# The third normalisation from group sums of the gated chunk and of its squares, gate times deviation spread once, and the last part re-staged over five rounds

## The chip, the cores and the metric

One core of one Trainium2 chip. The metric is the device time of one execution in microseconds; lower is better.

## The reference, cut to what matters

The input is 256 images of 256 channels on 7 x 7 positions. Four layers follow one another, each of them added to its input:

```python
x = x + _L0_conv_ref(_gn(x), ...)     # 1x1 convolution with gathered weights
x = x + _L1_conv_ref(_gn(x), ...)     # linear attention with a depthwise convolution
x = x + _L2_conv_ref(_gn(x), ...)     # spatial gate per group of 8 channels
x = x + _L3_conv_ref(_gn(x), ...)     # attention over the 49 positions of an image
```

`_gn` normalises every group of 8 channels of an image over its 8 x 49 values (32 groups, eps 1e-5). The change concerns the last two layers. The gate of the third one, for the normalised input v of a group: s is the sum of v over the 8 channels, the position of its maximum gives a vector q, and

```python
sim = (q . v) * D * zero + (mean over positions of v . v) * one
ctx = (sim - sim.mean()) / (sim.std(ddof=1) + 1e-05) * weight + bias
out = v * sigmoid(ctx)                # D: a gaussian around the maximum's position
```

The fourth layer, for its normalised input xf of an image (256 x 49):

```python
f, g, hh = Wq xf, Wk xf, Wv xf        # 32, 32 and 256 rows
beta = softmax(f^T g, axis=0)
out = gamma[0] * (hh beta) + xf
```

## The kernel before, in words

The kernel has a set-up, a phase for the first two layers (up to about 1588 us of the span, not touched) and `gate_and_attention_phase` (line 941), which does the last two. The first phase stores the normalised input of the gate layer (z2) in DRAM and keeps, per image and group, its mean (`gate_mean`), its standard deviation (`gate_std`) and its mean over the positions (`gate_gap`).

The last phase works on 16 chunks of 16 images. A chunk lies as 128 channels x 2 halves (t or m) x 784 columns (16 images x 49 positions). Group values lie in rows: 128 partitions stand for 4 quarters of the chunk x 32 groups, with 4 images x 49 = 196 columns. PE makes such rows from a chunk with 0/1 matrices (`sel`, "group sum": 8 matmuls) and spreads them back over the channels with `spread` (4 matmuls per half).

The phase is a software pipeline written out by hand. Every engine runs a loop of rounds (`rounds`); in round r a step with age k works on chunk r - k. The lists `v_round` (DVE), `pe_round`, `a_round` (ACT), `g_round` (POOL) and `sp_round` (SP, the queue of loads and stores) set the order of the steps on each engine; semaphores (`wait`, `done`) order the engines against each other. A step that waits holds everything behind it on its own engine. `v_then` makes a DVE step wait for its own result before the next one starts.

A chunk's way, with ages 0 to 6, so 22 rounds for 16 chunks: load z2 (0); group sums and search of the maximum (1, `pe_sums`, `v_find`); spread of the one-hot row, `v_picked`, `v_qv`, `v_prod` (2); the group sum of prod, `v_sim`, POOL's square root by a power (`g_deviation`), `v_context` (L1159 to L1163), tanh, `v_gate` (L1169), `v_gated` (L1173), `v_x3` (L1178), its sum per image and channel (`v_sum`, L1184) (3). Then the third normalisation, from x3 itself: `pe_mean` sums 8 channels (L1324), `v_centre` (L1188, L1192) subtracts the mean, ACT squares, `v_square_sum` (L1198) sums, `pe_var` (L1330), `v_var` (L1203), POOL's `g_root` on 128 x 32 values (L1511), `v_scale` (L1211) gives z3 (4 to 5). Then attention (5 to 6): `pe_fg`, `pe_scores`, `v_max` (L1220), exponentials on ACT, `v_probs` (L1227, L1228), `pe_turn`, `pe_hh`, `pe_out`, which adds z3 with an identity matmul (L1376, L1379), and `v_x4` (L1235), which adds x3 for the two halves m (x4a, x4b). SP stores the chunk.

POOL's other step is `g_gapped` (L1499), a product of a chunk with one value per image.

## Time and profile before

| | us |
|---|---|
| median of 3 runs | 2079.17 (2075.14 to 2084.48) |
| the profiled execution | 2083.96 |
| its span, first to last instruction | 2082.1 |
| the last phase in it | from about 1588 to 2082 |

Shares of the span: PE 86%, DVE 66%, ACT 43%, POOL 13%. These are means over three phases with different limits; the rows below are taken from the last phase alone. A busy time is the time in which the engine has an instruction in work; an instruction that is held inside its execution counts as busy, so a mean above the usual one for its size is a sign of holding. PEclk is the granted share of PE's clock. A row's "idle ... <-" names what ended the engine's idle time before it. Lines are those of the kernel before; tiles are named without their number, so z stands for z2 and z3 and x for x3 and x4.

### The profile page before, as it was taken

The page shows a single profiled execution, that of the slowest core. Times are in us where ns is not written, and L with a number is a line of the kernel's source. Part 1 is how long each engine was busy: PE and PEld are TensorE (multiplying, and loading weights), DVE is VectorE, ACT ScalarE, POOL GpSimd, SP SyncE. Part 2 cuts the span into 40 slices and gives each one's busy share as a digit, 9 for nine tenths or more (in the row PEclk, how much of TensorE's full clock was granted, in tenths as well). Part 3 has the DMA queues.
Part 4 walks back from the last instruction along what each step waited for, and adds up shares of the span by engine and source line. Part 5 has one row for each costly group of instructions (what it writes and reads, how often), then busy time and mean ns, then how long its engine had stood idle before and what let it go on. Part 6 is the DMA issues. An engine that isn't in the chain of part 4 may idle for free. (4 is left out here: it accounts for less than half of the span.)

```text
span 2082.1 us, 42128 instructions
## 1 busy us (share of the span) xinstructions
PE 1786.3 (86%) x16164; PEld 1195.1 (57%) x16164; DVE 1372.3 (66%) x2786; ACT 901.7 (43%) x2341; POOL 277.0 (13%) x189
## 2 busy tenths in 40 slices
PE   2699999999999999997877888999983499999998
PEld 1355555555555555565555666666661366666666
DVE  4677777666555556442333447777875899999994
ACT  0344454454554544453433445455541144444343
POOL 1000000001111101002111110000001233333331
PEclk9899999999999999998988899999995699999999
DMA  3112222237666667479988986545513001111101
GB/s 100 39 63 78 101 94 78 78 125 185 207 170 199 201 160 215 145 185 218 237 231 219 246 229 166 134 121 149 156 48 128 16 32 63 62 63 63 47 32 47
DMA packets 199916, 267.17 MB, mean 128 GB/s; under 512 B 108516, under 2 KB 159588, under 8 KB 199720
## 3 DMA queue, kind: packets, MB, share of 16 engines
q1 hardware_dynamic: 189320, 225.68, 38.4%
q10 hardware_dynamic: 10240, 38.54, 6.0%
q8 instruction: 132, 2.16, 0.4%
q14 instruction: 64, 0.52, 0.1%
q0 software_dynamic: 160, 0.26, 0.0%
HBM read 148.84 MB, written 115.61 MB: 127 GB/s over the span
## 5 line engine op out<-in xcount | busy, mean ns | idle before, releaser
L499 DVE TENSOR_TENSOR vk<-p_vk,mask_vo 128x512 f32<-128x512 f32 x256 | 176.4, 689 | 478.3 <-PE p_vk L392 478.3
L426 PE MATMUL p_dw<-tw,q 98*64 98x98 f32 x3072 | 198.3, 266 | 86.8 <-ACT agg_out L694 34.9
L834 POOL COPY q<-qd 98x768 f32<-98x768 f32 x128 | 110.5, 900 | 1085.5 <-DMA qd<-qkv_scratch 787.2
L667 ACT ACTIVATE half_b<-p_qkv 98x384 f32<-98x384 f32 x256 | 134.2, 524 | 244.2 <-PE p_qkv L351 229.6
L426 PEld LDWEIGHTS p_dw<-tw,q 98*64 98x64 f32 x3072 | 148.1, 143 | 151.5 <-issue 67.8
L694 ACT ACTIVATE agg_out<-p_dw 128x294 f32<-128x294 f32 x256 | 106.9, 417 | 258.6 <-PE p_dw L426 246.0
L452 PE MATMUL p_g<-o,w_proj 128*128 128x392 f32 x512 | 207.5, 531 | 3.4 <-DVE var L555 2.8
L351 PE MATMUL p_qkv<-w_qkv,half_a 128*98 128x384 f32 x512 | 193.8, 502 | 6.7 <-DVE half_a L571 6.7
L351 PE MATMUL p_qkv<-w_qkv,z_odd 128*98 128x384 f32 x512 | 190.2, 494 | 1.8 <-DVE z_odd L571 1.8
L404 PE MATMUL p_out<-vk,qr 128*49 128x136 f32 x2048 | 170.5, 287 | 8.5 <-DVE oN L514 5.4
L711 ACT ACTIVATE o<-p_turn 128x196 f32<-128x196 f32 x256 | 85.5, 334 | 167.5 <-PE p_turn L413 166.1
L1360 PE MATMUL p_b<-wv,z 128*98 128x256 f32 x512 | 121.2, 385 | 8.0 <-DVE x L1235 8.0
L413 PE MATMUL p_turn<-ident,oN 128*128 128x128 f32 x512 | 111.1, 300 | 19.1 <-ACT qr L686 17.4
L673 ACT ACTIVATE vT<-half_b,image_of 98x256 f32<-98x256 f32 x256 | 124.4, 538 | 0.0
L404 PEld LDWEIGHTS p_out<-vk,qr 128*49 128x49 f32 x2048 | 110.3, 125 | 24.3 <-issue 10.0
L452 PEld LDWEIGHTS p_g<-o,w_proj 128*128 128x128 f32 x512 | 91.8, 199 | 56.2 <-issue 16.8
L392 PEld LDWEIGHTS p_vk<-vT,kT 98*32 98x32 f32 x4096 | 71.6, 109 | 89.4 <-issue 85.0
L392 PE MATMUL p_vk<-vT,kT 98*32 98x66 f32 x4096 | 114.2, 228 | 3.4 <-DVE vk L503 3.2
L514 DVE TENSOR_TENSOR oN<-p_out,rden 128x256 f32<-128x256 f32 x256 | 108.6, 424 | 8.8
L351 PEld LDWEIGHTS p_qkv<-w_qkv,half_a 128*98 128x98 f32 x512 | 81.0, 174 | 57.4 <-issue 47.0
L351 PEld LDWEIGHTS p_qkv<-w_qkv,z_odd 128*98 128x98 f32 x512 | 79.8, 171 | 50.7 <-issue 44.9
L673 ACT ACTIVATE vT<-p_qkv,image_of 98x256 f32<-98x256 f32 x256 | 106.9, 474 | 0.0
(192 smaller groups left out, 3202.4 us busy)
## 6 DMA issues: line engine op xcount, KB each, us to landing
qkv_scratch<-half_b SPq DMA_DIRECT2D x32, 1176.0 KB
qd<-qkv_scratch SPq DMA_DIRECT2D x64, 588.0 KB
agg_scratch<-agg_out ACTq DMA_DIRECT2D x128, 294.0 KB, 5.8
tw<-in_w_toep SPq DMA_DIRECT2D x128, 220.5 KB
half_a<-agg_scratch SPq DMA_DIRECT2D x48, 392.0 KB, 6.9
half_b<-agg_scratch SPq DMA_DIRECT2D x48, 392.0 KB, 6.8
half_a<-in_x SPq DMA_DIRECT2D x16, 784.0 KB, 4.9
x_scratch<-xb SPq DMA_DIRECT2D x16, 784.0 KB, 4.8
```

The costliest lines, as they stand in the source:

```text
L351: mm = pe.matmul(p_qkv[r][0:PR, 0:QKV], z[c % 2][:, t, PR * w:PR * w + PR], W["w_qkv"][:, t, QKV * e:QKV * e + QKV], start=(t == 0), stop= ...
L392: mm = pe.matmul(p_vk[32 * c:32 * c + 32, 2 * VC * pr:2 * VC * pr + 2 * VC], kT[:, G % 2, pr, 32 * c:32 * c + 32], vT[:, G % 2, pr, :, c, ...
L404: mm = pe.matmul(out_of[64 * i:64 * i + S, pr, 0:VO], qr[:, G % 4, at:at + S], vk[:, G % 2, pr, i, :], start=True, stop=True)
L413: mm = pe.transpose(turned_of[:, pr, 0:128], oN[:, G % 2, pr, :], W["ident"][:, :])
L426: mm = pe.matmul(p_dw[NP * cp:NP * cp + NP, PR * s:PR * s + PR], q2[:, U % Q2, DB_CH * cp + 3 * (f % DB_FILLS) + s, :, :].rearrange("r w q ...
L452: mm = pe.matmul(bank[:, 0:HALF], W["w_proj"][:, q0 + e, 128 * m:128 * m + 128], o[:, n % 2, e, HALF * h:HALF * h + HALF], start=(e == 0), ...
L499: v.tensor_tensor(dst[:, :, 0:128].rearrange("p k (c n) -> p k c n", c=HC), src[:, :, 0:2 * D].unsqueeze(2).to_broadcast([128, 4, HC, 2 * D]),
L514: v.tensor_tensor(oN[:, G % 2, :, :].rearrange("p r (h d) -> p r h d", h=8), out_of[:, :, 0:128].rearrange("p r (h d) -> p r h d", h=8), r ...
L667: a.activation(raw[:, e, g % 4, :, r], p_qkv[r][0:PR, 0:QKV], ACT.Copy).then_inc(raw_ev, 1)
L673: a.activation(vT[:, G % 2, :, i, :, 0:2 * D], src.rearrange("r q (c n) -> r q c n", c=HC), ACT.Copy, scale=W["image_of"][:, i:i + 1]).the ...
L834: g.tensor_copy(q2[:, U % Q2, DB_CH * cp:DB_CH * cp + DB_CH, :, :].rearrange("r n w q -> r w n q"), qd[:, :, at:at + DB_CH, :]).then_inc(q ...
L1360: mm = pe.matmul(p_b[0:PR, n % 2, C * q:C * q + C], two_images(z3[it % Z3S][:, t, :], 2 * n + q), wv[:, t, :], start=(t == 0), stop=(t == ...
```

## The change

- The gated chunk's mean and variance per group are no longer taken from x3. As v * sigmoid + mean has the form (gate x z2) / 2 + constant inside a group, its moments are sums of gate x (group sum of z2) and gate^2 x (group sum of z2^2). ACT squares z2 at age 0 (`a_square`), `pe_sums` sums z2 and the squares, POOL weighs both rows (`g_weighed`), DVE sums them per image (`v_moment`) and makes the variance in group rows (`v_var`, 128 x 4), POOL takes the power (`g_root`, 128 x 4).
- The gate is multiplied with the reciprocal deviation in group rows (`v_gate_r`) and spread once; `v_zg` multiplies z2 by it. POOL adds a shift per image and channel (`g_shift`), which gives z3. The shift and the deviation come from `v_coef_rows`, one matmul pair (`pe_coef`) and `v_coef`.
- x3 is not kept. The residual of the fourth layer, x3 + z3, is zg x (1 + deviation) + base: half 0 on POOL (`g_rest`), half 1 on ACT in 16 short activations (`a_rest`). The identity matmuls leave `pe_out`.
- The softmax's reciprocal times gamma is a DVE step on 98 x 8 (`v_share`), the product is POOL's (`g_probs`).
- `pe_spread` and `pe_scores` use 64 rows of the array per matmul, alternating between the two halves of the rows. `sstd_eps` becomes a SCALAR_TENSOR_TENSOR with a tile of 1e-5.
- The ages are 0 to 4, with the store at 5: 21 rounds. All five lists have a new order. Four more constants are loaded ahead of the rounds.

The core of the diff (the rewritten operand forms of `v_find`, `v_dist` and `v_sim`, which keep their work, are left out, as are the declarations):

```diff
-    Z2S, X3S, Z3S = 5, 3, 3
+    Z2S, Z3S, ROWS = 6, 3, 4
...
         def v_context(v, it):
             wait(v, "sstd", it + 1)
-            v_then(v, it, v.tensor_scalar(sstd_eps[:, :], sstd[:, :], float((S - 1) ** -0.5), 1e-5,
-                                          ALU.mult, ALU.add), "sstd_eps")
+            v_then(v, it, v.scalar_tensor_tensor(sstd_eps[:, :], sstd[:, :], float((S - 1) ** -0.5), eps[:, :],
+                                                 ALU.mult, ALU.add), "sinv", 0, 2)
...
+        def v_moment(v, it):
+            wait(v, "weighed", 2 * it + 2)
+            done(v.tensor_reduce(moment[:, :, :].rearrange("g k b -> g (k b)"),
+                                 weighed[:, :, :].rearrange("g k (b s) -> g (k b) s", b=NQ), AX.X, ALU.add), "moment")
+        def v_var(v, it):
+            n = GS * S
+            wait(v, "moment", it + 1)
+            wait(v, "coef_rows", 2 * it)
+            v_then(v, it, v.tensor_scalar(mean[:, :], moment[:, 0, :], 0.5 / n, None, ALU.mult), "var_raw", 0, 3)
+            v_then(v, it, v.tensor_tensor(mean2[:, :], mean[:, :], mean[:, :], ALU.mult), "var_raw", 1, 3)
+            v_then(v, it, v.scalar_tensor_tensor(var[:, :], moment[:, 1, :], 0.25 / n, mean2[:, :],
+                                                 ALU.mult, ALU.subtract), "var_raw", 2, 3)
+            done(v.tensor_scalar(var[:, :], var[:, :], 0.0, 1e-5, ALU.max, ALU.add), "var_ok")
+        def v_gate_r(v, it):
+            wait(v, "rstd_ok", it + 1)
             wait(v, "gate_mm", 2 * it)
+            done(v.scalar_tensor_tensor(g_image(gate_r[:, :]), g_image(gate[:, :]), 0.5, g_over(rstd[:, :]),
+                                        ALU.mult, ALU.mult), "gate_r")
+        def v_coef_rows(v, it):
+            wait(v, "rstd_ok", it + 1)
+            wait(v, "coef_mm", it)
...
+            v_then(v, it, v.tensor_tensor(std[:, :], var[:, :], rstd[:, :], ALU.mult), "std", 0, 2)
+            v_then(v, it, v.tensor_tensor(rstd_of[:, :, :], by_quarter(rstd[:, :]), quarter[:, :, :], ALU.mult), "std", 1, 2)
+            done(v.scalar_tensor_tensor(coef_rows[:, 0, :, :], by_quarter(mean[:, :]), -1.0, rstd_of[:, :, :],
+                                        ALU.mult, ALU.mult), "coef_rows")
+            done(v.scalar_tensor_tensor(coef_rows[:, 1, :, :], by_quarter(std[:, :]), 1.0, quarter[:, :, :],
+                                        ALU.add, ALU.mult), "coef_rows")
+        def v_coef(v, it):
+            wait(v, "coef_mm", it + 1)
...
+            v_then(v, it, v.tensor_copy(c[:, :, :, :].rearrange("p t k b -> p (t k b)"), p_stat[:, 0:2 * KT * NB]), "coef", 0, 2)
+            done(v.tensor_tensor(base[it % 2][:, :, :], c[:, :, 0, :], W["gate_mean"][:, it, :, :], ALU.add), "coef")
-        def v_gated(v, it, t):
+        def v_zg(v, it, t):
             wait(v, "gate_mm", 2 * it + t + 1)
-            done(v.scalar_tensor_tensor(by_half(gx[:, t, :]), rows, 0.5, by_half(z2[it % Z2S][:, t, :]),
-                                        ALU.mult, ALU.mult), "gated")
+            done(v.tensor_tensor(by_half(zg[it % Z3S][:, t, :]), by_half(z2[it % Z2S][:, t, :]), rows, ALU.mult), "zg")
...
-            done(v.scalar_tensor_tensor(sc[:, :, :, :], sc[:, :, :, :], W["gamma"][0:PR, 0:1], over(srec[:, :, :]),
-                                        ALU.mult, ALU.mult), "probs")
+            done(v.tensor_scalar(share[:, :, :], srec[:, :, :], W["gamma"][0:PR, 0:1], None, ALU.mult), "share")
...
         def pe_spread(pe, sel_rows, src, t, name):
-            for q in range(4):
-                mm = pe.matmul(p_rows[:, q // 2, QC * (q % 2):QC * (q % 2) + QC], sel_rows[:, t, q, :], src[:, :],
-                               start=True, stop=True)
+            for q in (0, 2, 1, 3):
+                h = q // 2
+                mm = pe.matmul(p_rows[:, h, QC * (q % 2):QC * (q % 2) + QC], sel_rows[64 * h:64 * h + 64, t, q, :],
+                               src[64 * h:64 * h + 64, :], start=True, stop=True)
...
+        def pe_coef(pe, it):
+            wait(pe, "coef_rows", 2 * it + 2)
+            for t in range(KT):
+                mm = pe.matmul(p_stat[:, 2 * NB * t:2 * NB * t + 2 * NB], spread_all[:, t, :],
+                               coef_rows[:, :, :, :].rearrange("g k q b -> g (k q b)"), start=True, stop=True)
+            done(mm, "coef_mm")
...
         def pe_out(pe, it, m):
             for h in range(2):
                 wait(pe, "bt_ev", 2 * it + h + 1)
-                pe.matmul((p_a, p_b)[m][:, h, 0:HALF], W["ident"][:, :], z3[it % Z3S][:, m, HALF * h:HALF * h + HALF],
-                          start=True, stop=False)
...
+        def a_rest(a, it, part):
+            if part == 0:
+                wait(a, "shifted", 2 * it + 2)
+                wait(a, "coef", 2 * it + 2)
+            for b in range(NB // 4 * part, NB // 4 * part + NB // 4):
+                cols = zg[it % Z3S][:, 1, S * b:S * b + S]
+                done(a.activation(cols, cols, ACT.Identity, bias=base[it % 2][:, 1, b:b + 1],
+                                  scale=coef[it % 2][:, 1, 1, b:b + 1]), "rest_b")
...
+        def g_shift(g, it, t):
+            wait(g, "zg", 2 * it + t + 1)
+            wait(g, "coef", 2 * it + 1)
+            wait(g, "hh_mm", 4 * (it + 1 - Z3S))
+            done(g.tensor_tensor(by_b(z3[it % Z3S][:, t, :]), by_b(zg[it % Z3S][:, t, :]),
+                                 b_over(coef[it % 2][:, t, 0, :]), ALU.add), "shifted")
+        def g_rest(g, it):
+            cols = by_b(zg[it % Z3S][:, 0, :])
+            wait(g, "coef", 2 * it + 2)
+            done(g.tensor_tensor(cols, cols, b_over(coef[it % 2][:, 0, 1, :]), ALU.mult), "rest_a")
+            wait(g, "rest_a", 2 * it + 1)
+            done(g.tensor_tensor(cols, cols, b_over(base[it % 2][:, 0, :]), ALU.add), "rest_a")
...
-            run(g_root, 6)
-            run(g_deviation, 4)
-            run(g_gapped, 2)
+            run(g_deviation, 2)
+            run(g_shift, 3, 1)
+            run(g_weighed, 2)
+            run(g_root, 2)
+            run(g_gapped, 0)
+            run(g_rest, 3)
+            run(g_probs, 3)
+            run(g_shift, 2, 0)
...
-            for r in range(chunks + 6):
+            for r in range(chunks + 5):
```

The whole of `v_x3`, `v_sum`, `v_centre`, `v_square_sum` and `v_scale` is removed. The new order of a round, each step with its age and its half or part:

- DVE: var 3; picked 2, half 1; coef_rows 3; max 4; gate_r 3; qv 2; coef 3; prod 2; share 4; dsum 2; zg 3, half 0; sim 2; hot 1; ssq 2; zg 3, half 1; dist 1; context 2; picked 1, half 0; gate 2; x4 4, half 0; find 0; x4 4, half 1; moment 2.
- PE: turn 4; sums 0; hot 1, half 0; out 4, both halves; fg 3; hot 1, half 1; hh 3, part 0; scores 3; hh 3, part 1; coef 2; hh 3, part 2; gate 2, half 0; hh 3, part 3; sim 1; gap 0; gate 2, half 1.
- SP: load 0; store 5 (before: store 6, load 0).

## Rows read from the trace of the kernel before

**Rows 1.** Windows: stretch, its length, busy us of each engine (instructions), PEclk, DMA.

```profile
1746.33:1773.53 27.20, 24.70 (x183) 17.83 (x182) 26.68 (x40) 11.21 (x34) 10.00 (x3) 1.00 0.18 61
```

**Rows 2.** Timelines of PE and DVE: start, us, engine, line, op, out<-in, count, idle.

```profile
1598.74 1.53 PE L1274 MATMUL p_sum<-z,sel 128*32 128x196 f32 x16 [2.61 <-DMA z<-z_scratch]
...
1693.92 0.97 DVE L1235 TENSOR_TENSOR x<-p_b,x 128x784 f32<-128x784 f32 x1
...
1993.11 0.97 DVE L1235 TENSOR_TENSOR x<-p_b,x 128x784 f32<-128x784 f32 x1
...
2077.34 0.97 DVE L1235 TENSOR_TENSOR x<-p_b,x 128x784 f32<-128x784 f32 x1 [2.13 <-PE p_b L1379]
```

**Rows 3.** Groups by form, 1740 to 1900, DVE: busy us, mean ns | idle before.

```profile
L1211 DVE TENSOR_TENSOR z<-zc,rstd 128x784 f32<-128x784 f32 x12 | 11.6, 968 | 0.0
...
L1159 DVE TENSOR_SCALAR sstd_eps<-sstd 128x4 f32<-128x4 f32 x6 | 11.4, 1905 | 0.0
L1192 DVE TENSOR_TENSOR zc<-x,mean 128x1568 f32<-128x1568 f32 x6 | 10.8, 1792 | 0.2
L1184 DVE TENSOR_REDUCE stat<-x 128x32 f32<-128x1568 f32 x6 | 10.7, 1786 | 0.2
L1178 DVE TENSOR_TENSOR x<-gx,gate_mean 128x1568 f32<-128x1568 f32 x6 | 10.7, 1783 | 0.0
L1198 DVE TENSOR_REDUCE stat<-sq 128x32 f32<-128x1568 f32 x6 | 10.7, 1778 | 0.0
...
L1228 DVE SCALAR_TENSOR_TENSOR sc<-sc,gamma,srec 98x784 f32<-98x784 f32 x6 | 6.2, 1034 | 0.2
```

**Rows 4.** The same view, small steps of DVE.

```profile
L1169 DVE TENSOR_TENSOR gate<-tanh,one_std 128x196 f32<-128x196 f32 x6 | 2.2, 359 | 0.0
...
L1105 DVE TENSOR_TENSOR below<-last,row_ends 128x24 f32<-128x24 f32 x6 | 1.1, 176 | 0.0
```

**Rows 5.** Timelines of POOL and DVE in the first rounds, POOL beside DVE.

```profile
1603.31 3.00 DVE L1099 TENSOR_TENSOR hot_exact<-hot,last 128x196 bf16<-128x196 f32 x1
...
1621.05 2.81 POOL L1499 TENSOR_TENSOR gapped<-z,gate_gap 128x1568 f32<-128x1568 f32 x1
...
1621.09 2.79 DVE L1159 TENSOR_SCALAR sstd_eps<-sstd 128x4 f32<-128x4 f32 x1 [0.29 <-POOL sstd L1505]
...
1667.06 2.82 POOL L1499 TENSOR_TENSOR gapped<-z,gate_gap 128x1568 f32<-128x1568 f32 x1
...
1667.46 4.06 DVE L1192 TENSOR_TENSOR zc<-x,mean 128x1568 f32<-128x1568 f32 x1
```

**Rows 6.** POOL's powers: timeline of a late round, and the group by form.

```profile
2000.90 5.43 POOL L1511 TENSOR_TENSOR rstd<-var,minus_half 128x32 f32<-128x32 f32 x1 [5.47 <-DVE var L1203]
...
2004.30 1.04 DVE L1228 SCALAR_TENSOR_TENSOR sc<-sc,gamma,srec 98x784 f32<-98x784 f32 x1
...
L1505 POOL TENSOR_TENSOR sstd<-ssq,plus_half 128x4 f32<-128x4 f32 x6 | 6.0, 1007 | 72.9 <-DVE ssq L1155 72.9
```

**Rows 7.** Timeline of PE and its weight loads (PEld) in steady rounds.

```profile
1741.78 0.85 PE L1376 MATMUL p_a<-z,ident 128*128 128x392 f32 x2
1742.14 1.19 PEld L1379 LDWEIGHTS p_a<-beta,hh 98*128 98x128 f32 x8
...
1743.33 0.85 PE L1376 MATMUL p_b<-z,ident 128*128 128x392 f32 x2
...
1760.43 1.56 PE L1281 MATMUL p_rows<-gate,spread 128*128 128x196 f32 x8
```

**Rows 8.** Timeline of PE, then the window around it (columns as rows 1).

```profile
1639.52 0.38 PE L1324 MATMUL p_stat<-stat,mask 128*128 128x32 f32 x2 [3.83 <-DVE sim L1143]
...
1639.00:1642.00 3.00, 0.96 (x10) 0.75 (x14) 2.43 (x7) 0.68 (x2) 0.57 (x1) 0.63 0.00 0
```

**Rows 9.** Groups by form, 1740 to 1900, ACT.

```profile
L1436 ACT ACTIVATE tanh<-sim,half_par 128x196 f32<-128x196 f32 x6 | 3.3, 550 | 3.9 <-DVE sim L1163 3.9
```

**Rows 10.** Timeline of SP, constant loads ahead of the rounds.

```profile
1591.65 0.43 SPq L1554 DMA_DIRECT2D wqk<-in_wqk  x1
```

More of the change, by code:

```diff
@@ L968, in gate_and_attention_phase @@
         pick = sb("pick", [128, KT, COLS])
-        gx = sb("gx", [128, KT, COLS])
         gapped = sb("gapped", [128, KT, COLS])
-        zc = sb("zc", [128, KT, COLS])
         sq = sb("sq3", [128, KT, COLS])
-        stat = sb("stat3", [128, 2, KT * NB])
-        mean = sb("mean3", [128, KT, NB])
-        var = sb("var3", [128, KT * NB])
-        rstd = sb("rstd3", [128, KT, NB])
+        sums = [sb(f"sums_{i}", [128, 2, QC]) for i in range(ROWS)]
+        gate2 = sb("gate2", [128, QC])
+        weighed = sb("weighed", [128, 2, QC])
+        moment = sb("moment", [128, 2, NQ])
+        mean = sb("mean3", [128, NQ])
+        mean2 = sb("mean2", [128, NQ])
+        var = sb("var3", [128, NQ])
+        rstd = sb("rstd3", [128, NQ])
+        std = sb("std3", [128, NQ])
+        rstd_of = sb("rstd_of", [128, 4, NQ])
+        coef_rows = sb("coef_rows", [128, 2, 4, NQ])
+        coef = [sb(f"coef_{i}", [128, KT, 2, NB]) for i in range(2)]
+        base = [sb(f"base_{i}", [128, KT, NB]) for i in range(2)]
+        gate_r = sb("gate_r", [128, QC])
         qv = sb("qv", [128, KT, NB])
@@ L1029, in gate_and_attention_phase @@
         p_b = ps("p_b", [128, 2, 512])
-        names = """consts params logged std_mm met_sp met_g
-            s_mm s_ev gapped gap_mm gap_ev best at_best counted last hot below row col apart dist2 gauss dsum
-            hot_mm picked qv prod sim_mm sim_max sim ssum sim_centred sim_squared ssq sstd sstd_eps sinv context
-            tanh gate_ok gate_mm gated x3 sum_ok mean_mm mean_ok centred squared square_sum var_mm var_ok rstd_ok z3
-            fg_mm fg_ev score_mm smx neg_max exp srec probs hh_mm hh_ev bt_mm bt_ev o_mm x4a x4b""".split()
+        names = """consts params logged std_mm met_sp
+            sq_ok s_mm s_ev gapped gap_mm gap_ev found last hot placed apart gauss dsum
+            hot_mm picked qv prod sim_mm sim sim_centred sim_squared ssq sstd sinv context
+            tanh gate_ok gate2 weighed moment var_raw var_ok rstd_ok gate_r std coef_rows coef_mm coef
+            gate_mm zg shifted rest_a rest_b fg_mm fg_ev score_mm neg_max exp share probs hh_mm hh_ev
+            bt_mm bt_ev o_mm x4a x4b""".split()
         sems = {name: sem("p2_" + name) for name in names}
@@ L1304, in pe_hot @@
             if t == 0:
-                wait(pe, "gated", 2 * it - 2)
+                wait(pe, "zg", 2 * it - 2)
             else:
@@ L1311, in pe_gate @@
         def pe_gate(pe, it, t):
-            wait(pe, "gate_ok", it + 1)
+            wait(pe, "gate_r", it + 1)
             if t == 0:
@@ L1316, in pe_gate @@
             else:
[L1317 to L1330 removed]
+                wait(pe, "zg", 2 * it + 1)
+            pe_spread(pe, spread, gate_r, t, "gate_mm")
+        def pe_coef(pe, it):
[4 more added lines that the diff above has]
+            done(mm, "coef_mm")
         def pe_fg(pe, it):
[L1333 removed]
+            wait(pe, "shifted", 2 * it + 2)
             wait(pe, "x4a", it)
@@ new lines, in a_fg, with a_exp @@
+        def a_fg(a, it, h):
+            wait(a, "fg_mm", it + 1)
+            wait(a, "score_mm", it)
+            for k, dst in enumerate((f_sb, g_sb)):
+                done(a.activation(dst[2 * G * h:2 * G * h + G, :], p_a[2 * G * h + G * k:2 * G * h + G * k + G, 0, 0:HALF],
+                                  ACT.Copy), "fg_ev")
+        def a_exp(a, it, h):
+            wait(a, "neg_max", 2 * it + 2)
+            wait(a, "bt_mm", 2 * it)
+            wait(a, "share", 2 * it - 1)
+            for q in range(4):
+                done(a.activation(sc[:, h, q, :], scores[:, h, q, :], ACT.Exp, bias=neg_max[:, h, q:q + 1],
+                                  accum_out=ssm[:, h, q:q + 1]), "exp")
```

318 lines of the change are left out of this document (152 added, 166 removed).

## The prediction

> **What bounds the kernel now.** I read the windows by stage first, then the starts of one step that comes once a round, then the groups of instructions by form, and last the timelines of VectorE (DVE) and GpSimd (POOL) side by side. The change touches only the third phase. In a steady round of it DVE is busy 26.68 of 27.20 us, TensorE (PE) 24.70, ScalarE (ACT) 11.21, POOL 10.00, and the granted clock is 1.00, the 2.4 GHz level [rows 1]. So DVE sets the pace, and PE is only 10% behind it.
>
> The phase is a pipeline. The second half of a chunk's output (x4b) is the last step of the chunk. Its first start is 1693.92, the twelfth 1993.11, the sixteenth 2077.34; the first group sums start at 1598.74 [rows 2]. So the first chunk needs 95.2, eleven steady rounds take 299.2 (27.20 each), the four last rounds 84.2, and 4.8 remain to the end of the span at 2082.1: 1598.7 + 95.2 + 299.2 + 84.2 + 4.8 = 2082.1. I make the new sum in these five terms.
>
> **What leaves DVE.** Per round: x3 (1.78), its sum (1.79), the centring (1.79), the sum of squares (1.78), two scalings (2 x 0.97), the product with the softmax's reciprocal (1.03, now POOL's) [rows 3], and two steps on 128x32, taken at 0.18 as the 128x24 step [rows 4]: 10.5. A further loss is hidden in L1159: a TENSOR_SCALAR on 128x4 takes 1.905 on average [rows 3], against some 0.17 for its size [rows 4], so 1.74 of it is waiting; that is taken up below.
>
> **What comes to DVE.** Eleven steps on 4 to 64 elements (four for mean and variance, four for the coefficient rows, two for the coefficients, one for the softmax share) at 0.18 = 2.0; gate_r, 196 elements, 0.36 [rows 4]; the moment, 392 elements, between 0.36 (196) and 0.97 (784) [rows 3, 4], 0.56 by interpolation. Together 2.9. The gated product stays at its price. So DVE's own work is 26.68 - 1.74 - 10.5 + 2.9 = 17.3, and 18.0 with 0.7 for the gaps that steps waiting for their predecessor leave (0.5 in the round of before [rows 1], with more such steps now).
>
> **What DVE then waits for.** The rows show that POOL and DVE stop each other. gapped ran 1667.06 to 1669.88; the centring, which reads two SBUF operands, started at 1667.46 and took 4.06 instead of 1.79, so it ended 1.64 after gapped. And when the pow ended at 1621.05, gapped started at 1621.05 and the DVE step that waited for the pow at 1621.09: it took 2.79 [rows 5]. POOL's pow does not hold DVE: a 1.04 step with two SBUF operands ran at 2004.30 inside a pow of 5.43 [rows 6].
>
> The Trainium skill, "SBUF — State Buffer", section "Who interferes with whom", says the same and more: the port pair that both share is an exclusive lock, held for the whole instruction, and a DVE instruction with two SBUF inputs contends for it with a GpSimd instruction that reads SBUF. It speaks against this change, which gives POOL seven more such instructions a round. On gapped the trace agrees (4.06 for 1.79), on the pow it does not (1.04 inside 5.43). By the rule without that exception the two pows of a round would hold DVE too, up to 2.0 more; the sum goes by the rows.
>
> The new POOL work: two shifts, the rest's multiply and add, the softmax product (784 elements each), two weighings (196). gapped has 1568 elements at 2.82 [rows 5]; half of it is 1.41. With a fixed cost per instruction, 0.37 from the two pow sizes (1.007 for 4 columns, 5.43 for 32) [rows 6], it is 1.60. I take 1.45, near the plain half, as gapped is the same kind of step. The pow of the root falls from 5.4 (32 columns) to 1.0 (4 columns). POOL's round is then some 13, never the bound by itself.
>
> The Trainium skill, "GPSIMD Engine Reference", section "3.1 Elementwise — side-by-side cycle accounting", gives two-input steps about 2.6 cycles an element, which is an estimate of 1.70 for 784 elements; by it gapped would take 3.40, and the row has 2.82. With 1.70 the round below would be about 0.9 longer.
>
> Now the order of the new round. DVE starts with the four variance steps (to 0.9), POOL takes the root (0.9 to 1.9), and right behind it in its queue gapped (1.9 to 4.7), then the rest's multiply and add. DVE meanwhile takes picked and comes to std, which reads var and rstd and waits for the root: it becomes ready at the very moment gapped starts, as the step at 1621.09 did, and is held 2.8. Its two successors each wait for the one before, POOL gets in between with 1.45 each. That group costs 5.6 whichever of the two wins a tie. Later shift 0 meets the centring of sim (0.7), shift 1 the row search (1.1), the second weighing the find (0.2). Stalls: 7.6. Where DVE waits for ACT or PE (best for the sums, ssq for the squares, the mean for the moment) I count 1.2. **Round: 18.0 + 7.6 + 1.2 = 26.8, taken as 26.9.** The new DVE wait on the root holds everything behind it on DVE: max, gate_r, qv, prod; and PE's coef, which holds hh 2, gate 0, hh 3 and sim.
>
> **What lies beside it.** PE: the identity matmuls of the output go (0.85 of a group that begins every 1.55; the eight weight loads of 1.19 stay and pace the rest [rows 7]), 4 x 0.36 = 1.4 saved; the group sum of the squares comes, 1.53 at the half clock [rows 2], so 0.8: 24.1; that two small matmul pairs become one I leave out. Whether matmuls on two halves of the array's rows run together no row shows; if the two gate groups of 1.56 [rows 7] did, PE would be at 22.6, if they gained nothing 24.1. DVE's 26.9 covers both. ACT: 16 short activations with two per-partition operands and the squares of the gate, at most 0.55 each as tanh, which has two such operands and 196 elements where most of these have 49 [rows 9], and the longer sums 0.2: at most 11.2 + 9.6 = 20.8. Covered; if DVE's round fell below that it would show. SP: four more constant loads ahead of the first chunk, at most 0.43 each [rows 10]: +1.6 once. The z load waits for zg instead of gated, six buffers deep, and the store now stands behind the load in SP's queue; with the load's wait five chunks back neither is late.
>
> **The sum.** The first chunk: x4b came in the seventh round, after six rounds in 95.2 (15.9 each); it now comes at the end of the fifth: 5 x 15.9 = 79. Start 1598.7 + 1.6; first chunk 79; eleven rounds of 26.9 = 296; the four last rounds 84, taken as before, since fewer chunks are in flight there and PE's work keeps nearly its size; 4.8. Together **2066**, 16 under the span of 2082.1. The profiled execution itself took 2083.96, which is 4.8 above the median of the runs, 2079.17; 16 less than that median is **2063**. Most of the gain is the shorter pipeline, little of it the 9 us that DVE is spared.
>
> **Rivals.**
> 1. *DVE's short steps slip past POOL* (four elements held for 2.8 are shown only for a TENSOR_SCALAR, not for a step with two tensors). Then DVE needs 19.2 and PE paces the round at 22.6 to 24.1: 1600.3 + 72 + 11 x 23.3 + 79 + 4.8 = 2012 for the span (a stall of some 1.4 less in each of the first five rounds, and PE's saving in the last four), about 2009 for the median, and 1995 or less if the hot and score groups, split in the same way, gain too. For: a step that small was never seen against gapped in the two-operand form. Against: the centring's 4.06, the 3.00 of a two-operand step of 196 elements that is otherwise near 0.36, and 2.79 for four elements [rows 5].
> 2. *A longer hold or a slower clock eats the rest.* With 1.60 a POOL step the round is 27.6. And PE idles 3 to 4 us before coef (in the order above its hh 1 ends near 4, the coefficient rows come near 7.8): in the trace an idle of 3.83 stands before a window with a mean granted clock of 0.63, part of it at the 1.2 GHz level [rows 8]; that would put sim and gate some 1.5 later, to 28.4. Median 2068 to 2082: no measurable change.
> 3. *Slower: all of POOL's shared-port time lands on DVE.* POOL's steps that hold the port sum to 2.8 + 5 x 1.45 + 2 x 0.4 = 10.9. If POOL's next step always goes before a waiting DVE step, and each meets one, the round is 18.0 + 10.9 + 1.2 = 30.1: 1600.3 + 79 + 331 + 84 + 4.8 = 2099, median about 2095. It decides against the change from 29.5 a round on (2092.5, which is 10.4 over 2082.1). For: POOL's steps are spread over the whole DVE queue. Against: DVE spends about 9 us of the round in eight steps that read PSUM or reduce (seven of 784 elements, one of 1568, at the prices of rows of that size [rows 3]), and some POOL time must fall there.
>
> **How the numbers follow.** Forecast (2052 to 2068) 0.45; rival 1 and what lies between it and the forecast 0.22; rival 2 0.20; rival 3 0.13. The likeliest is 2063. The range takes rival 1 from 1995 and rival 3's lower part, to 2090, leaving about 1 in 10 outside on each side. What a measurement of this kernel can tell from no change is about 0.5% (10.4 us). Faster by more: forecast and rival 1, 0.67; within: rival 2, 0.20; slower: rival 3, 0.13.
>
> **What would show it.** In the changed kernel's profile: std, four elements, with a mean near 2.8 and the next two near 1.4, means the hold is as told; near 0.2 means rival 1. x4b spaced 26.9 in steady rounds, the first 79 after the first group sums. POOL's 784-element steps between 1.41 and 1.60 where DVE does not hold them. PE's gate groups at 0.8 or 1.56 tell whether the halves run together. A granted clock under 1.00 in steady rounds speaks for rival 2, a round of 29.5 or more for rival 3. The prediction fails at its root if DVE is no longer the engine that the round waits for.

## The result and the profile after

The changed kernel takes 2058.51 us (median of 6 runs, 2052.93 to 2064.51), the kernel before, beside it on the same chip, 2079.35 (6 runs, 2073.96 to 2084.48): a ratio of 0.9914, 95% interval 0.9889 to 0.9940. The prediction was 2063, range 1995 to 2090. The profiled execution of after took 2054.89, with a span of 2053.1.

The five terms of the prediction's sum, read from the same starts as in [rows 2]. Timeline of after: start, us, engine, line, operation, out<-in, what ended the idle before.

```profile
1589.71 1.54 PE L1296 MATMUL p_sum<-z,sel 128*32 128x196 f32 x16 [2.65 <-DMA z<-z_scratch]
...
1664.38 0.98 DVE L1259 TENSOR_TENSOR x<-p_b,zg 128x784 f32<-128x784 f32 x1
...
1965.14 0.96 DVE L1259 TENSOR_TENSOR x<-p_b,zg 128x784 f32<-128x784 f32 x1
...
2048.23 0.97 DVE L1259 TENSOR_TENSOR x<-p_b,zg 128x784 f32<-128x784 f32 x1 [0.81 <-PE p_b L1398]
```

| term, us | before | predicted | after |
|---|---|---|---|
| first group sums to first x4b | 95.2 | 79 | 74.7 |
| eleven steady rounds | 299.2 | 296 | 300.8 |
| last four rounds | 84.2 | 84 | 83.1 |
| to the end of the span | 4.8 | 4.8 | 4.9 |
| the whole stretch | 483.4 | 464 | 463.4 |

The stretch is 20.0 shorter (483.4 - 463.4), and the medians differ by 20.8. All of it is the first term, 20.5; a steady round is not shorter but 0.14 longer: 27.34 (300.8 / 11) for 27.20. The two spans differ by 29, 9 of which lie before 1589.71, in code that the change doesn't touch; the first group sums move that much from execution to execution (they start at 1588.5 to 1604.2 in the traces of this document), so kernels are compared here from their first group sums on, or by medians.

A steady round of after, windows (columns as in [rows 1]: stretch, length, then PE, PEld, DVE, ACT, POOL, the granted clock and DMA): the whole round, then one window of 1 us in it.

```profile
1773.70:1801.00 27.30, 22.02 (x188) 15.48 (x188) 24.68 (x44) 16.59 (x52) 13.48 (x10) 0.94 0.17 60
...
1784.70:1785.70 1.00, 1.00 (x4) 0.58 (x3) 1.00 (x1) 1.00 (x6) 0.00 (x0) 0.50 0.03 8
```

Against [rows 1], DVE is busy 24.68 instead of 26.68, PE 22.02 instead of 24.70, ACT 16.59 instead of 11.21, POOL 13.48 instead of 10.00, and the granted clock is 0.94, with a stretch at 0.50, the 1.2 GHz level. No engine is full, and the round is as long as before. Where it goes is in the same round's timelines of POOL, DVE and PE:

```profile
1776.99 2.82 POOL L1536 TENSOR_TENSOR gapped<-z,gate_gap 128x1568 f32<-128x1568 f32 x1
1779.77 1.50 POOL L1573 TENSOR_TENSOR zg<-zg,coef 128x784 f32<-128x784 f32 x1
1781.35 1.53 POOL L1575 TENSOR_TENSOR zg<-zg,base 128x784 f32<-128x784 f32 x1
...
1777.05 2.78 DVE L1218 TENSOR_TENSOR std<-var,rstd 128x4 f32<-128x4 f32 x1 [0.26 <-POOL rstd L1554]
1779.86 1.44 DVE L1219 TENSOR_TENSOR rstd_of<-rstd,quarter 128x16 f32<-128x16 f32 x1
1781.34 0.17 DVE L1220 SCALAR_TENSOR_TENSOR coef_rows<-mean,rstd_of 128x16 f32<-128x16 f32 x1
1781.43 1.48 DVE L1222 SCALAR_TENSOR_TENSOR coef_rows<-std,quarter 128x16 f32<-128x16 f32 x1
...
1790.71 0.42 DVE L1158 SCALAR_TENSOR_TENSOR sim<-p_stat,half_zero,dsum 128x196 f32<-128x196 f32 x1 [1.16 <-issue]
...
1782.96 0.63 PE L1349 MATMUL p_stat<-coef_rows,spread_all 128*128 128x32 f32 x4 [3.45 <-DVE coef_rows L1222]
1783.43 3.32 PE L1381 MATMUL p_b<-wv,z 128*98 128x256 f32 x8
...
1787.81 1.97 PE L1381 MATMUL p_b<-wv,z 128*98 128x256 f32 x8
...
1791.17 0.93 PE L1304 MATMUL p_rows<-gate_r,spread 64*128 64x196 f32 x8
```

Read the starts and the ends: std (4 elements) ends with gapped, rstd_of (16) ends with the rest's multiply, the second coefficient row with the rest's addition. These three take 5.70 where 0.5 would do. PE's coef waits 3.45 for the last of them; behind that wait the clock is 0.50, the next hh group takes 3.32 instead of 1.97, and DVE waits 1.16 before sim. So a chain that starts with a POOL instruction of no urgency comes back to DVE 13 us later.

### The profile page after: what moved, and what is told of

Its sections match the earlier page's. It is cut to its first block and busy times, and to the rows that moved or that the text cites. A ratio compares the mean times of both kernels' runs of the same rounds, so it can differ in the third digit from the quotient of the medians.

```text
span 2053.1 us, 42896 instructions
## 1 busy us (share of the span) xinstructions
PE 1729.0 (84%) x16292; PEld 1150.4 (56%) x16292; DVE 1331.2 (65%) x2851; ACT 988.1 (48%) x2613; POOL 335.9 (16%) x301
## 5 line engine op out<-in xcount | busy, mean ns | idle before, releaser
L452 PE MATMUL p_g<-o,w_proj 128*128 128x392 f32 x512 | 201.7, 518 | 3.4 <-DVE var L555 2.9
L1381 PE MATMUL p_b<-wv,z 128*98 128x256 f32 x512 | 144.7, 433 | 16.5 <-DVE x L1259 16.0
L1381 PEld LDWEIGHTS p_b<-wv,z 128*98 128x98 f32 x512 | 88.5, 183 | 52.1 <-issue 24.9
```

Source lines behind the costliest of these rows:

```text
L452: mm = pe.matmul(bank[:, 0:HALF], W["w_proj"][:, q0 + e, 128 * m:128 * m + 128], o[:, n % 2, e, HALF * h:HALF * h + HALF], start=(e == 0), ...
L1381: mm = pe.matmul(p_b[0:PR, n % 2, C * q:C * q + C], two_images(z3[it % Z3S][:, t, :], 2 * n + q), wv[:, t, :], start=(t == 0), stop=(t == ...
```

## The experiments

Theory A is: POOL's long two-operand instructions hold (stop and lengthen) DVE's steps that have two SBUF operands or are a TENSOR_SCALAR, and this sets the round; the gain of the change is the shorter passage of the first chunk alone. Each expectation sets its own theory B against it. Rounds are the distances of x4b in the traces.

**e1: POOL waits for the coefficient rows before gapped.**

```diff
             wait(g, "gap_mm", it)
+            wait(g, "coef_rows", 2 * it - 2)
```

> One edit: POOL waits for both coefficient rows of the chunk two back before it starts gapped. Now gapped runs 2.8 right behind the root, and std, rstd_of and the second coefficient row take 2.78, 1.44 and 1.48 on DVE instead of some 0.17 each: 5.2 of a round of 27.34. Theory A (POOL's instruction holds DVE, and with it PE's coef): the three fall to 0.2 or less, PE's wait of 3.45 before coef is gone and the granted clock of a steady round is back at 1.00, and DVE's wait of 1.16 before sim goes too. Part returns, because gapped then runs beside the maximum (0.96, reads PSUM) and meets neg_max and gate_r, 1.8 at most, and the rest's two steps meet base and prod, 1 at most. Round 27.34 - 5.2 - 1.2 + 1.8 + 1 = 23.7 to 25.5, first chunk 5 to 6 shorter, median about 2010 to 2032. Theory B (the hold is only handed on: whichever two-operand step comes next takes all of gapped): neg_max or gate_r takes 2.8, the round stays between 26.5 and 28, median within 10 of 2058.

Measured: median 2034.12, ratio to before 0.9769 (0.9726 to 0.9811). Seven of the eleven rounds take 25.0 to 25.3, four 26.3 to 27.0 (mean 25.7, just above theory A's 25.5); the median lies 2 above its range. Timeline of DVE, POOL and PE of e1:

```profile
1769.17 0.16 DVE L1218 TENSOR_TENSOR std<-var,rstd 128x4 f32<-128x4 f32 x1 [0.26 <-POOL rstd L1555]
...
1769.67 0.17 DVE L1222 SCALAR_TENSOR_TENSOR coef_rows<-std,quarter 128x16 f32<-128x16 f32 x1
...
1770.79 2.07 DVE L1243 TENSOR_SCALAR neg_max<-smx 98x8 f32<-98x8 f32 x1
...
1770.01 2.82 POOL L1537 TENSOR_TENSOR gapped<-z,gate_gap 128x1568 f32<-128x1568 f32 x1 [0.87 <-DVE coef_rows L1222]
...
1785.42 3.73 PE L1398 MATMUL p_a<-beta,hh 98*128 98x98 f32 x16
...
1811.85 2.03 PE L1398 MATMUL p_a<-beta,hh 98*128 98x98 f32 x16
```

The three steps take 0.16 to 0.17, and PE's wait before coef is gone. A wait added to POOL takes 2.0 to 2.4 off the seven short rounds. There is a second effect: in every round PE now waits 1.9 before the group sums, because ACT's eviction of gap_sim comes late. In the long round read closely the output group behind that wait took 3.73 at the low clock; in the short round after it, behind the same wait, it took 2.03. The granted clock is back at 1.00, as theory A had it, in only three of the eleven rounds. Theory B, that the hold is merely handed on, holds in part: neg_max takes 2.07, to the end of gapped, and sim's second step 1.78 instead of 0.53.

**e2: rstd_of doesn't wait for std.**

```diff
-            v_then(v, it, v.tensor_tensor(std[:, :], var[:, :], rstd[:, :], ALU.mult), "std", 0, 2)
+            done(v.tensor_tensor(std[:, :], var[:, :], rstd[:, :], ALU.mult), "std")
```

> One edit: rstd_of no longer waits for std, which it doesn't read. Theory A (the prediction's step: the successor of a held step is held again because it waits for its predecessor, and POOL gets in between): rstd_of follows std at once and takes 0.17 to 0.2; 1.3 of its 1.44 goes, round 26.1 if nothing takes its place, or the hold moves to the first coefficient row, which still waits (0.18 to 1.4, round unchanged within 0.3). Theory B (POOL's next instruction already stands ready and goes before DVE's next one, wait or no wait, as the second coefficient row, which waits for nothing, was held 1.48): rstd_of stays at 1.4, round 27.3.

Measured: median 2044.04, ratio 0.9837 (0.9799 to 0.9876); every round 26.2. Timeline of e2, from two rounds:

```profile
1771.28 2.78 DVE L1218 TENSOR_TENSOR std<-var,rstd 128x4 f32<-128x4 f32 x1 [0.26 <-POOL rstd L1554]
1773.98 0.16 DVE L1219 TENSOR_TENSOR rstd_of<-rstd,quarter 128x16 f32<-128x16 f32 x1
1774.17 1.36 DVE L1220 SCALAR_TENSOR_TENSOR coef_rows<-mean,rstd_of 128x16 f32<-128x16 f32 x1
1775.46 0.16 DVE L1222 SCALAR_TENSOR_TENSOR coef_rows<-std,quarter 128x16 f32<-128x16 f32 x1
...
1783.02 1.78 DVE L1161 TENSOR_TENSOR sim<-sim,gap_sim 128x196 f32<-128x196 f32 x1
...
1809.62 0.42 DVE L1158 SCALAR_TENSOR_TENSOR sim<-p_stat,half_zero,dsum 128x196 f32<-128x196 f32 x1 [0.77 <-issue]
1810.08 0.93 DVE L1161 TENSOR_TENSOR sim<-sim,gap_sim 128x196 f32<-128x196 f32 x1
```

Without its wait rstd_of follows the held std at once and passes; the next step, which waits, lets POOL in. So the prediction's "POOL gets in between" is right for rstd_of. It is not a rule for every step that waits: in after the first coefficient row waits for rstd_of too, and starts 0.01 before POOL's addition (1781.34 against 1781.35), with 0.17. The hold moved to the first coefficient row, as theory A allowed, but the round didn't stay the same: the second row then passed, which the expectation hadn't said. Of three holds two are left, PE's wait before coef is 1.95 instead of 3.45, and in the round shown the granted clock is 1.00 and the wait before sim is gone. Part is taken back at once: sim's second step now meets the softmax product and the shift on POOL, 1.78 instead of 0.53. In four of the eleven rounds the clock does fall behind coef's wait (mean 0.93). There DVE waits 0.72 to 0.77 before sim, and the hold of the second step is as much shorter (0.92 to 0.98), since it ends with the shift on POOL: these rounds take 26.2 as well.

**e3 and e6: filler matmuls in PE's wait before coef, eight and five.**

```diff
+            wait(pe, "picked", min(2 * it + 4, 2 * chunks))
+            for k in range(8):
+                pe.matmul(p_rows[:, 0, 0:HALF], W["ident"][:, :], z2[it % Z2S][:, 0, 0:HALF], start=True, stop=True)
             wait(pe, "coef_rows", 2 * it + 2)
```

> One edit: eight matmuls of 392 columns, whose result nobody reads, fill the wait of PE before coef (3.45 idle, after which the granted clock is 0.50 to 0.57 for about 3 and PE's next three groups take some 1.7 longer). Theory A (the low clock is the cause of DVE's wait of 1.16 before sim): the granted clock of a steady round returns to 1.00, that wait falls under 0.2, the round is 26.1 to 26.4, median about 2043 to 2048. Theory B (the low clock is covered, the wait before sim comes from the late coefficient rows): wait and round stay within 0.3 of 1.16 and 27.34. If the filler itself runs past the coefficient rows, coef starts up to 0.5 later.

Measured for e3: median 2071.36, ratio 0.9960 (0.9939 to 0.9982), rounds 27.33. The filler ran 5.43, past the coefficient rows: coef came 1.7 late, so the wait of 1.07 before sim, with the clock at 1.00, can't tell the theories apart. The 13 more than after lie in the first passage (77.1) and the last four rounds (94.0). e6 repeats it with `range(5)`.

> The changed kernel with five filler matmuls in PE's wait before coef instead of eight: the eight took 5.43 and made coef 1.7 late, so that DVE's wait before sim stayed at 1.07 although the granted clock was back at 1.00. Five take 3.4, the length of the wait. Theory A (the low clock makes DVE wait before sim): clock 1.00, that wait under 0.2; the round falls, but as in e2 the second step of sim may then meet POOL's softmax product and shift (1.78 for 0.53), so between 26.1 and 27.3. Theory B: the wait stays near 1.16 with the clock at 1.00.

Measured for e6: median 2066.61, ratio 0.9922 (0.9895 to 0.9949), rounds 27.3 to 27.4, just above the range given; the 8 more than after lie in the last four rounds (92.5 for 83.1). Timelines of PE and DVE of e6, then windows of 1 us:

```profile
1789.50 3.45 PE L1348 MATMUL p_rows<-z,ident 128*128 128x392 f32 x10
...
1793.56 1.95 PE L1384 MATMUL p_b<-wv,z 128*98 128x256 f32 x8
...
1803.48 1.40 PE L1296 MATMUL p_sum<-z,sel 128*32 128x196 f32 x16 [1.90 <-ACT gap_sim L1439]
...
1799.60 0.42 DVE L1158 SCALAR_TENSOR_TENSOR sim<-p_stat,half_zero,dsum 128x196 f32<-128x196 f32 x1
1800.05 1.79 DVE L1161 TENSOR_TENSOR sim<-sim,gap_sim 128x196 f32<-128x196 f32 x1
```

```profile
1794.00:1795.00 1.00, 1.00 (x6) 0.75 (x6) 1.00 (x3) 0.83 (x5) 0.00 (x0) 1.00 0.00 0
...
1804.00:1805.00 1.00, 1.00 (x19) 0.83 (x15) 0.93 (x4) 0.11 (x1) 1.00 (x2) 0.50 0.00 0
```

With the clock held at 1.00 behind coef the hh group takes 1.95 and DVE no longer waits before sim: the low clock was the cause of that wait. It is worth nothing to the round, because the 1.16 are taken over by the hold of sim's second step (1.79 instead of 0.53), and the clock falls later in the round, behind a wait of 1.90.

**e4: the gate spread over all 128 rows again.**

```diff
-            pe_spread(pe, spread, gate_r, t, "gate_mm")
+            for q in (0, 2, 1, 3):
+                mm = pe.matmul(p_rows[:, q // 2, QC * (q % 2):QC * (q % 2) + QC], spread[:, t, q, :], gate_r[:, :],
+                               start=True, stop=True)
+            done(mm, "gate_mm")
```

> One edit: the spread of the gate goes back to all 128 rows, so its two matmuls of one pair no longer run on two halves of the array. Theory A (halves run together, and the first gate group stands in the chain from coef to sim): the second gate group, at full clock, takes 1.5 to 1.6 instead of 0.9, the first 2 or more instead of 1.20, DVE's wait before sim grows by 0.6 to 0.9, round 27.9 to 28.2, median 2067 to 2072. Theory B (PE is not in the chain): the groups are longer, the round stays 27.3.

Measured: median 2063.79, ratio 0.9932 (0.9905 to 0.9960), nine of eleven rounds 27.5. Timeline of e4:

```profile
1798.62 1.59 PE L1344 MATMUL p_rows<-gate_r,spread 128*128 128x196 f32 x8
...
1798.16 0.42 DVE L1158 SCALAR_TENSOR_TENSOR sim<-p_stat,half_zero,dsum 128x196 f32<-128x196 f32 x1 [1.49 <-issue]
```

The second group behaves as said (1.59 for 0.93 at full clock): two matmuls on two halves of the rows do run together, since a single one takes 0.33 in both kernels and only their starts lie closer in after (eight within 0.6 instead of 1.3). The first group takes 1.49, not 2 or more. It is worth only 0.15 in these nine rounds (the other two take 27.8 and 29.1), and round and median lie under theory A's ranges: the wait before sim grew by 0.33, not 0.6 to 0.9, and sim's second step, coming later, lost its hold of 0.17. PE is in the chain, but with little weight.

**e7: one round more in the pipeline.** Every step of the attention one age later, with a fourth zg and z3 (the list is shortened).

```diff
-        Z2S, Z3S, ROWS = 6, 3, 4
+        Z2S, Z3S, ROWS = 6, 4, 4
...
-            run(v_max, 4)
+            run(v_max, 5)
...
-            run(pe_fg, 3)
+            run(pe_fg, 4)
```

> The changed kernel with every step of the attention (hh, f and g, scores, maximum, exp, share, probabilities, transposes, output, last sum) one round later and one buffer more for zg and z3; the work of a round and its order stay. Theory A (the prediction's: the gain is the number of rounds that the first chunk passes, some 15 each in the filling pipeline): first x4b 87 to 93 after the first group sums instead of 74.7, steady rounds 27.1 to 27.6, median 2069 to 2078, most of the 20 given back. Theory B (the gain is the shorter chain of one chunk's steps, not the number of rounds): first x4b at most 80, median within 6 of 2058.

Measured: median 2073.37, ratio 0.9962 (0.9935 to 0.9989). Timeline of e7:

```profile
1602.41 0.88 PE L1296 MATMUL p_sum<-z,sel 128*32 128x196 f32 x8 [2.41 <-DMA z<-z_scratch]
...
1701.36 0.97 DVE L1259 TENSOR_TENSOR x<-p_b,zg 128x784 f32<-128x784 f32 x1
1728.68 0.96 DVE L1259 TENSOR_TENSOR x<-p_b,zg 128x784 f32<-128x784 f32 x1
...
2073.96 0.97 DVE L1259 TENSOR_TENSOR x<-p_b,zg 128x784 f32<-128x784 f32 x1 [0.81 <-PE p_b L1398]
```

The round is the same, 27.32 (1728.68 - 1701.36). The first x4b comes 99.0 after the first sums, 24 more than in after and more than said, and 11 of that return at the end, where one more round runs short: 9 in the last four rounds (74.1), 2 in the round before them. From the first sums to the last x4b it is 471.6 for 458.5 in after: 13 given back by this alone, 15 in the medians. So a round of passage is worth two thirds to three quarters of what the change brought.

**e8: the kernel before, with POOL waiting.** As e1, in the kernel before: gapped waits for the normalised sim.

```diff
             wait(g, "gap_mm", it)
+            wait(g, "context", it - 1)
```

> The kernel before with one edit: POOL waits for the normalised sim of the chunk two back before it starts gapped, which so no longer runs beside sstd_eps (1.90 for some 0.17) but beside the sum of squares and the row search. Theory A (the hold costs the old formulation the same way): sstd_eps takes 0.2, the round falls from 27.2 by 1.2 to 1.8 to 25.4 to 26.0 (PE needs 24.7), median 2055 to 2066, as much as the whole change brought. Theory B (the hold moves to the next two-operand step of the row search, 0.36 now): round 26.8 to 27.4, median within 8 of 2079.

Measured: median 2065.50, ratio 0.9919 (0.9894 to 0.9945); rounds 26.32. Timeline of e8:

```profile
1747.97 0.16 DVE L1159 TENSOR_SCALAR sstd_eps<-sstd 128x4 f32<-128x4 f32 x1
...
1750.83 1.12 DVE L1090 TENSOR_TENSOR hot<-s_sb,best 128x196 f32<-128x196 f32 x1
```

sstd_eps falls from the 1.90 of [rows 3] to 0.16, but the end of gapped now catches hot (1.12 for 0.36): 0.88 a round is left of 1.74, so the round misses theory A's 25.4 to 26.0, while the median lies just inside its range. One line in the old formulation brings 14 us, where the whole change brings 21.

**e5, e9, e10, e11: how far it goes.** e5: gapped waits for gate_r, which moves ahead of the maximum; neg_max moves behind qv; gap_sim gets two buffers and its eviction stands ahead of sim's squares (the lines for these two, and the split of neg_max from the maximum, are left out here).

```diff
+            wait(g, "gate_r", it - 1)
...
-            run(v_max, 4)
             run(v_gate_r, 3)
+            run(v_max, 4)
             run(v_qv, 2)
+            run(v_neg, 4)
```

> The version of e1 taken further. gapped waits for gate_r, which now comes right behind the coefficient rows, and the maximum and the sum qv, 0.97 (PSUM) and 1.77 (a reduction), stand beside gapped's 2.82; neg_max comes behind them. gap_sim has two buffers and its eviction stands ahead of the squares of sim on ACT, since in e1 PE waits 1.91 for it before the group sums, and in 4 of 11 rounds the groups behind that wait ran at a granted clock of 0.5 (the first output group 3.73 for 2.03; those rounds take 27.0 for 25.0). Theory A (only the coincidence of POOL's and DVE's two-operand steps costs, and what it costs can be placed beside PSUM and reduction steps): neg_max falls from 2.07 to 0.4 or less, the wait before the group sums goes, no round falls to the low clock, all rounds within 23.0 to 24.3, median 1995 to 2012. Theory B (the hold moves on to the next step): neg_max, base or prod take it, rounds 25 or more, median 2025 or more.

Measured for e5: median 2022.01, ratio 0.9715 (0.9683 to 0.9747); nine rounds 24.5, two 25.1 and 25.4. neg_max falls to 0.52, nearly the 0.4 said, but the round missed its range by 0.2 and the median by 10, since other steps are held. The low clock came back too, in two rounds (mean 0.90 and 0.91), and the round behind each of them is one of the two long ones. Timeline of e5:

```profile
1815.04 1.32 DVE L1232 TENSOR_TENSOR base<-coef,gate_mean 128x32 f32<-128x32 f32 x1
1816.28 1.78 DVE L1142 TENSOR_TENSOR prod<-z,qv 128x1568 f32<-128x1568 f32 x1
1818.13 0.20 DVE L1250 RECIPROCAL srec<-ssm 98x8 f32<-98x8 f32 x1
1818.37 1.08 DVE L1251 TENSOR_SCALAR share<-srec,gamma 98x8 f32<-98x8 f32 x1
...
1820.96 1.78 DVE L1161 TENSOR_TENSOR sim<-sim,gap_sim 128x196 f32<-128x196 f32 x1
...
1816.39 3.03 POOL L1579 TENSOR_TENSOR zg<-zg,base 128x784 f32<-128x784 f32 x1
```

Here POOL is stopped too: its addition starts 0.11 after prod and needs 3.03 instead of 1.50, 1.5 more, about what prod takes. Inside it the RECIPROCAL passes with 0.20, the TENSOR_SCALAR waits for its end. e9 is e5 with sim's second step reading the gap sums from PSUM; ACT's eviction goes, and gapped and its group sum come a round later (only the step itself is shown).

```diff
-            v_then(v, it, v.tensor_tensor(sim[:, :], sim[:, :], gap_sim[it % 2][:, :], ALU.add), "sim", 1, 3)
+            v_then(v, it, v.scalar_tensor_tensor(sim[:, :], p_sum[:, 0:QC], W["g_par"][:, 2:3], sim[:, :], ALU.mult, ALU.add), "sim", 1, 3)
```

> The version of e5 with one step of the similarity changed: its second step, which adds gap_sim from SBUF and was held for 1.78 by POOL's softmax product and first shift, now reads the gap sums straight from PSUM and multiplies by the parameter in the same instruction; ACT's eviction goes, and gapped and its group sum come a round later. Theory A (a DVE step with one operand in PSUM is not held, as picked and zg, 0.96 each, never were): the step takes 0.42 or less although POOL runs beside it; the fourth step, two SBUF operands, is then held until the shift ends, 0.8 at most; round 24.5 - 1.4 + 0.8 = 23.7, between 23.4 and 24.0. Theory B (any DVE step with two operands is held): it stays at 1.5 or more, round 24.3 to 24.7.

Measured for e9: median 2011.49, ratio 0.9680 (0.9657 to 0.9704), rounds 23.71, as said. Timeline of e9:

```profile
1817.06 0.42 DVE L1161 SCALAR_TENSOR_TENSOR sim<-p_sum,g_par,sim 128x196 f32<-128x196 f32 x1
...
1817.91 0.94 DVE L1163 SCALAR_TENSOR_TENSOR sim<-ssum,sim 128x196 f32<-128x196 f32 x1
...
1817.13 1.50 POOL L1571 TENSOR_TENSOR z<-zg,coef 128x784 f32<-128x784 f32 x1
```

Beside the same POOL instruction the step with one operand in PSUM takes 0.42, and the one with two in SBUF (0.36 in after) is held: it ends at 1818.85, 0.22 after POOL's. e10 is e5 with the rest's steps at other places in POOL's list, and DVE's first x4 ahead of the gate (that move is left out here).

```diff
         def g_rest(g, it):
...
+            wait(g, "context", min(it + 2, chunks))
...
+        def g_rest_add(g, it):
...
+            wait(g, "last", min(it + 4, chunks))
...
+            run(g_rest, 3)
             run(g_weighed, 2)
+            run(g_rest_add, 3)
...
-            run(g_rest, 3)
```

> The version of e5 with the rest's two POOL steps taken from behind gapped, where they hold base (1.32 for 0.19) and share (1.08 for 0.23) and the second itself needs 3.03 for 1.50 because prod runs: the multiply now waits for the normalised sim and stands beside pick 0 and the first half of the output (1.93 on DVE, both PSUM; this half now ahead of the gate), the addition waits for the last row search and stands beside the second half and the moment (1.52, PSUM and a reduction). Theory A (what costs is the coincidence alone): base 0.2, share 0.25, round 24.5 - 1.9 + 0.3 = 22.7 to 23.2, median about 1990 to 2002. Theory B (POOL's steps always cost DVE their length somewhere): gate, the row search or the variance steps take 1 to 2 instead, round 24 or more.

Measured for e10: median 2012.06, ratio 0.9666 (0.9641 to 0.9691), rounds 23.70: between the 22.7 to 23.2 of theory A and theory B's 24, the median 10 above theory A's. base takes 0.19 and share 0.23, but DVE now waits 1.20 for ACT's exponentials before srec, a wait that the holds had hidden, and sim's second step is still held (1.62). e11 has both edits.

> e9 and e10 together. Theory A: the two savings add, 24.5 - 0.8 - 1.6 = 22.1, between 21.6 and 22.8; PE's busy time of 20.2 at full clock is the next bound, and only where no wait of PE brings the low clock back; median 1965 to 1990. Theory B (PE's chain from the maximum through the transposes to the output now sets the round): at most 0.4 under the better of the two.

Measured for e11: median 2001.43, ratio 0.9623 (0.9604 to 0.9642), rounds 22.9: 0.1 above the range given, the median 11 above it. e9 and e10 each take 0.8 off the 24.5 of e5, and together 1.6: the two savings add, which theory B (at most 0.4 under the better of the two) doesn't allow. A steady round of e11, windows:

```profile
1787.38:1810.30 22.92, 20.30 (x188) 14.53 (x188) 20.00 (x44) 16.28 (x51) 13.51 (x10) 1.00 0.21 72
```

DVE is busy 20.0 of 22.9, PE 20.30 at full clock, POOL does the same work as in after. This version beats both kernels: its median is 80 under that of before beside it (2081.35), and 57 under after's.

## Why the prediction was right, and where its steps were off

**The order of the gains was right, and for most of it the reason given.** "Most of the gain is the shorter pipeline": the passage is 20.5 shorter, the whole stretch 20.0. That the number of rounds does it is shown by e7 for 13 of these. The passage was priced too high, at 79: a round was priced from before (15.9), and it is 14.9 (74.7 / 5).

**The round: each part, and what failed.** The forecast was 18.0 own + 7.6 stalls + 1.2 waits, taken as 26.9; measured is 27.33 = 18.46 own + 6.94 stalls + 1.93 waits (before std 0.26, sim 1.16, ssq 0.16, best 0.35).

- The group behind the root: "costs 5.6", measured 2.78 + 1.44 + 1.48 less three usual durations, 5.2. The mechanism is shown by e1 (all three gone) and e2 (the wait lets POOL in). Which successors are held was half wrong: rstd_of and the second row, not the first, which starts 0.01 before POOL's addition.
- The smaller stalls: the row search 1.21 (said 1.1), the find 0.37 (0.2), sim 0.17 where 0.7 was said for its centring. Groups by form of after, 1740 to 1900, mean ns of one:

```profile
L1218 DVE TENSOR_TENSOR std<-var,rstd 128x4 f32<-128x4 f32 x6 | 16.7, 2776 | 1.6 <-POOL rstd L1554 1.6
...
L1123 DVE SCALAR_TENSOR_TENSOR at_row<-at_row,last 128x4 f32<-128x4 f32 x6 | 8.2, 1372 | 0.2
...
L1567 POOL TENSOR_TENSOR z<-zg,coef 128x784 f32<-128x784 f32 x12 | 18.0, 1498 | 0.0
...
L1547 POOL TENSOR_TENSOR weighed<-gate,sums 128x196 f32<-128x196 f32 x6 | 3.6, 600 | 13.1 <-DVE gate L1184 13.1
```

- POOL's step of 784 elements: 1.45 taken, bounds 1.41 and 1.60, measured 1.50. The weighing, 0.60 for 0.4: between the two sizes there is a fixed part, which the plain half left out.
- Waits: 1.93 instead of 1.2. What was counted (best, ssq, moment) came to 0.51, and the root cost 0.26 before std; the term that failed is the wait before sim, 1.16. It was in the text, but as rival 2's case (PE idle before coef, low clock, "1.5 later"), while the forecast counted nothing for it. The mechanism came in full, with PE idle for 3.45 and the hh group at 3.32; only its price for DVE was smaller. e6 and four rounds of e2 show that nothing would have been won by avoiding it alone, since a hold stands ready to take its place.
- DVE's own work: 18.46, 0.5 more than counted.
- What lies beside it: ACT 16.59, under the 20.8 allowed, with 0.43 on average for a short activation of the rest where at most 0.55 was said (0.550 in [rows 9]); the gate groups 0.93 for the 1.56 of [rows 7]; the start 0.2 later against the first constant load (10.02 for 9.83) instead of 1.6.

The Trainium skill, "SBUF — State Buffer", section "Who interferes with whom", says that TENSOR_SCALAR, where its operands allow it, can enter a mode that uses both port pairs and so contend with GpSimd, that a reduction on trn2 never does, and that a step with at most one SBUF input, outside those modes, stays clear. The traces agree: neg_max 2.07 (e1) and share 1.08 (e5) are held, qv beside gapped is not (1.78 in e5), nor is sim from PSUM (0.42 in e9).

**The rivals.** Rival 1 (short steps slip past POOL) is refuted by std's 2776. Its time of 2009 with the PE-bound round of 23.3 came near only where POOL's work was moved, in e9 and e10 (rounds of 23.7, medians of 2011 and 2012). Rival 2 is true as a mechanism, at a part of its price (1.16 for 1.5). Rival 3 needed all of POOL's port time to land on DVE: 2.82 + 1.50 + 1.53 + 1.54 + 2 x 1.50 + 2 x 0.60 = 11.6. 6.9 came. The rest fell beside PSUM and reduction steps, as the argument against it said, or into DVE's wait before sim.

**Luck, a slip, and what stays open.** That the sum was only 1 off the stretch of 463.4 is partly luck: passage and last four were 5 too long, the rounds 5 too short. The prediction's last addition has a slip: its terms, 1600.3 + 79 + 296 + 84 + 4.8, make 2064, not 2066, which would have given a median of 2061; neither the range nor the order of the gains hangs on it. The gain beyond e7's 13 was not traced to a step. e7 passes as many rounds as before and still stays 7 under it from the first sums to the last x4b. Its passage is not shorter (99.0 for 95.2), but its last four rounds are (74.1 for 84.2). So a shorter chain of one chunk's own steps does not show in its passage, and why its end is shorter was not read.

## What to carry to other kernels

An engine that is busy for half of the round can still set it: look for DVE steps whose duration is far above their size, and see which POOL instruction ends with them. Then give POOL a wait, so that its long instruction starts beside DVE steps that read PSUM or reduce; and before taking one stall away, look for the next that stands behind it. In a pipeline of few chunks, count rounds of passage too: one round less was worth 13 to 15 us here, while the work spared on DVE, some 8 a round by the prediction's count (10.5 less 2.9), brought nothing as long as POOL's holds took its place. With most of them moved (e11), the eleven rounds are 47 shorter than before's.
